# Three edits to a transformer block's kernel: an 8-bit copy of the quantised values, later attention transposes, later waits for right factors

## The chip, the cores and the metric

The kernel runs on one core of one Trainium2 chip. The metric is the device time of one execution in microseconds. TensorE (PE) does the matrix products and the transposes, VectorE (DVE) and ScalarE (ACT) the elementwise work, SyncE (SP) issues most of the DMAs, and GpSimd (POOL) does six reductions across partitions. Each engine works through its own list of instructions in order. What one engine needs from another is guarded by semaphores: an instruction that waits holds back all that stands behind it in the list of its engine.

## The reference, cut to what matters

`x` has 16 batches of 64 tokens of 1024 numbers. Three blocks, each fed with the layernorm of `x`, are added to it one after another.

```python
x = x + xattn(layernorm(x), ctx, ctx, ...)     # cross attention over 1601 context rows, batch norm
x = x + attn(layernorm(x), Wq, Wk, Wv, Wo, ...)
x = x + ffn(layernorm(x), W1, b1, W2, b2)

# attn: 8 heads with two softmax maps each
q = (x @ Wq).reshape(B, T, 8, 2, 64); k = (x @ Wk).reshape(B, T, 8, 2, 64)
v = (x @ Wv).reshape(B, T, 8, 128)
o = softmax(mask(q0 k0^T)/8) v - lam * softmax(mask(q1 k1^T)/8) v
o = o * rsqrt(mean(o*o) + eps) * g * (1 - LAMBDA_INIT)
out = o.reshape(B, T, E) @ Wo

# ffn: weights made ternary (alpha * sign(W) where |W| > 0.05 max|W|), then
y = gelu(x @ W1q.T + b1) @ W2q.T + b2
scale = max|y| / 7 + 1e-8
out = clip(round(y / scale), -7, 7) * scale
```

## The kernel before, in words

The kernel is written by hand as one list of instructions for each engine. The order inside each list is the order of the code. The 1024 tokens lie in `NT = 8` tiles of 128 partitions, and the 1024 features in `NC = 8` chunks.

**Attention.** The loop over the heads `h` runs from 0 to `H - 1 = 7` and is a software pipeline: while PE makes the queries and keys of head `h`, the softmax and the weighing of the values of head `h - 1` pass through DVE and ACT. The queries and keys of a head come from seven block products (a scheme in the manner of Strassen), `qk_product(h, m)` with `m` from 0 to 6 (line 943), each of four f32 matrix instructions of 512 columns, which the profile counts as eight records. Product 0 goes to PSUM bank 0, 1 to bank 1, 2 to bank 0, 3 to bank 2, 4 to bank 0, 5 to bank 3, 6 to bank 0. Between them PE does three pieces for the head before: `turn(h)` transposes the attention weights `a_bd` (line 953), `weigh(h)` multiplies them by the values (line 963), and `put_oT(h)` transposes the normalised result (line 971). Then `scores(h)` makes the 64 small score products (line 982): its start waits for DVE's last collection of the head (`dve_part`), its second half for ACT's copy `part(h, 6)` (`act_part >= 3h + 3`).

The list of ACT for one head is: `exps(h)` (line 615, with a table load ahead of it), `part(h, 0)` and `part(h, 1)` (copies of products 0 and 1 out of PSUM, line 639), `count(4h)`, `put_aT(h)` (line 620), `squares(h)` (line 626, then a table load and a small square root at line 628), `count(4h + 1)`, `count(4h + 2)`, `part(h, 6)`, `put_oT(h)` (line 633), `count(4h + 3)`. A `count` is three passes over a 128x1024 tile of W1 (lines 607, 609, 611).

The list of DVE for one head is: `shift(h)` (lines 1368 to 1371), `right_sum_4(h)`, `ternary(4h)` (lines 1325 and 1326), `combine(h)` (lines 1375 to 1383, the last of which writes `a_bd`), `collect_qk(h, 0)`, `ternary(4h + 1)`, `collect_qk(h, 1)`, `ternary(4h + 2)`, `normal(h)` (line 1387 to 1393; inside it `collect_qk(h, 2)`), `right_sums(h + 1)`, `collect_qk(h, 3)`, `ternary(4h + 3)`. A collection (line 1403) adds a bank of PSUM to the queries or keys.

`ternary(n)` needs the tile `n` of W1 in one of two buffers `w_buf`. SP loads tile `n + 2` into the buffer of tile `n` (line 424) when `count(n)` is done.

**The product with W2.** It is also made from seven block products, `product(r, s)` with `r` from 0 to `7 * HK - 1 = 111` and four row groups `s` (line 1075). Step `r` needs a left factor in the ring `hl` (written by ACT and DVE) and a right factor in the ring `t_half` of 8 slots, which SP loads from DRAM when step `r - 8` is done (line 480). `operands(r)` holds the two waits. The last eight steps are ordered the other way round: all eight for `s = 0`, then all eight for `s = 1`, and so on, so that DVE can collect row group 0 while PE does the others (lines 1527 and 1531).

**The end.** DVE and POOL find the largest `|y|` over all. For each of the 8 tiles the value `y / scale` is then rounded by adding `ROUND = 1.5 * 2**23` and taking it off again, multiplied by the scale and added to `xo2`. ACT does the first pass for tiles 1 to 7 (line 709) and DVE for tile 0 (line 1557). Taking `ROUND` off is done by ACT for the tiles in `Q_ACT = (2, 4, 6, 7)` (line 713) and by DVE for 0, 1, 3 and 5 (line 1563). DVE multiplies and adds (line 1565), and SP stores each tile to DRAM (line 504).

Of the kernel before, what the change touches and what calls it, by code (L numbers as in the profile page):

```python
# [26 lines left out]

F32 = mybir.dt.float32
F16 = mybir.dt.float16
ALU = mybir.AluOpType  # L30
ACT = mybir.ActivationFunctionType
AX = mybir.AxisListType
# [2 lines left out]
P = 128  # L35
B, C, N = 16, 64, 1024
M = 1601
NT = B * C // P
# [32 lines left out]
ROUND = 1.5 * 2.0 ** 23  # L71
QMAX = 7.0
Q_ACT = (2, 4, 6, 7)
H_ORDER = [(hc, j) for j in range(2) for hc in range(4)] + [(hc, j) for hc in range(4, HC) for j in range(2)]
HK = HC // 2
RING = 12
BRING = 8
LAST_K = 8
# [27 lines left out]
def build(nc, x, ctx, ctxT_in, small_w, wqk, wv, wo, lambdas, w1t, w2t, b2, consts, out):  # L106
    with ExitStack() as stack:
# [3 lines left out]
        def sb(name, shape, at, dt=F32):  # L111
            return nc.alloc_sbuf_tensor_at(name, shape, dt, offset=BASE + at)

        KB = 1024
# [23 lines left out]
        x2T = sb("x2T", [P, NC, NT * P], 84 * KB)  # L138
        t_out = sb("t_out", [P, 2, 1024], 116 * KB, F16)
        tok = sb("tok", [P, NT, N], 120 * KB)  # L140
# [9 lines left out]
        x3s = [sb("x3s0", [P, N], 48 * KB), sb("x3s1", [P, N], 116 * KB)]  # L150
        x3h = sb("x3h", [P, NC, NT * P], 160 * KB, F16)
        x3l = sb("x3l", [P, NC, NT * P], 176 * KB, F16)

        w2_buf = sb("w2_buf", [P, 2, 1024], 0)
        t2_set = sb("t2_set", [P, 2, 8, BANK], 8 * KB, F16)
        hl = sb("hl", [P, RING, 2, BANK], 0, F16)
        t_half = sb("t_half", [P, BRING, BANK], 24 * KB, F16)
        hq = sb("hq", [P, 4, HK, BANK], 32 * KB)
        xo2 = sb("xo2", [P, NT, N], 96 * KB)
        y = sb("y", [P, NT, N], 160 * KB)  # L160
        t_buf = sb("t_buf", [P, 4, 1024], 192 * KB, F16)
        b2_bc = sb("b2_bc", [P, N], 200 * KB)

        at = [204 * KB]

        def small(name, shape):
            n = 4 * int(np.prod(shape[1:]))
            t = sb(name, shape, at[0])
            at[0] += n + (-n) % 32
            return t  # L170
# [25 lines left out]
        ym = small("ym", [P, 24])  # L196
# [82 lines left out]
        whole_ready = sem("whole_ready")  # L279
        z_ready, q_ready, d_vec, out_stored = sem("z_ready"), sem("q_ready"), sem("d_vec"), sem("out_stored")  # L280
# [29 lines left out]
        def width(mt):  # L310
            return P if mt < MT - 1 else TAIL
# [213 lines left out]
        def _(act):  # L525
            A = act.activation
# [17 lines left out]
            for p in range(NT):  # L544
# [3 lines left out]
                for e, pair in enumerate(pairs(p)):  # L548
                    n = BANK if pair[0] == "wide" else 4 * width(pair[0])
# [32 lines left out]
            for hf in range(2):  # L582
                f = slice(hf * BANK, hf * BANK + BANK)
# [101 lines left out]
            for m, (hc, j) in enumerate(H_ORDER):  # L685
# [5 lines left out]
                if m >= 1 and H_ORDER[m - 1] in T2_AFTER:  # L691
                    n = T2_AFTER[H_ORDER[m - 1]]
# [12 lines left out]

            act.wait_ge(d_vec, 2)

            def rounded(t):
                A(y[:, t, :], y[:, t, :], ACT.Copy, scale=ym[:, 20:21], bias=ROUND).then_inc(z_ready, 1)

            def whole(t):
                act.wait_ge(z_ready, t)
                A(y[:, t, :], y[:, t, :], ACT.Copy, bias=-ROUND).then_inc(whole_ready, 1)

            for t in range(NT):
                if t > 0:
                    rounded(t)
                if t in Q_ACT:
                    whole(t)


        @block.tensor
        def _(pe):
# [193 lines left out]
            def qk_product(h, m):  # L917
                b = (0, 1, 0, 2, 0, 3, 0)[m]
                if m == 0:
                    pe.wait_ge(wqk_in[(h + 1) % 2], 16 * (h // 2) + 16)  # L920
                    if h:
                        pe.wait_ge(act_part, 3 * h)
                if h == 0 and m in (0, 1, 3, 5):
                    pe.wait_ge(v_out, 2 * NT - 3 + b)
                if h == 0 and m in (1, 2, 4, 5):
                    pe.wait_ge(xs_sum, 4 * (1, 2, 4, 5).index(m) + 4)
                if m == 1:
                    pe.wait_ge(tw_ready, 4 * h + 3)
                if m == 2:
                    pe.wait_ge(act_part, 3 * h + 1)  # L930
                if m == 3 and h:
                    pe.wait_ge(dve_part, 4 * h - 2)
                if m == 4:
                    pe.wait_ge(dve_part, 4 * h + 1)
                if m == 5 and h:
                    pe.wait_ge(dve_part, 4 * h)
                if m == 6:
                    pe.wait_ge(dve_part, 4 * h + 3)
                    pe.wait_ge(tw_ready, 4 * h + 4)
                fresh = m in (0, 1, 3, 5)  # L940
                for c in range(4):
                    right, left = factors(h, m, c)
                    ins = mm(bank(b), right, left, start=(fresh and c == 0), stop=(c == 3), skip_group_check=not fresh)  # L943
                ins.then_inc(m_done, 1)
# [40 lines left out]

            pe.wait_ge(x2_out, 2 * NT)
            for h in range(H):
                for m in range(3):
                    qk_product(h, m)
                if h:  # L990
                    turn(h)
                qk_product(h, 3)
                if h:
                    weigh(h)
                for m in range(4, 7):
                    qk_product(h, m)
                if h:
                    put_oT(h)
                    pe.wait_ge(on_ready, h)
                scores(h)  # L1000
# [64 lines left out]
            def product(r, s):  # L1065
                m, k = r // HK, r % HK
                b = 4 * (m % 2) + s
                if k == 0:
                    if m < 2:
                        pe.wait_ge(g_ready, 2 * HC - 7 + b)  # L1070
                    else:
                        pe.wait_ge(y_out, 4 * (m - 2) + s + 1)
                fresh = m in (0, 1, 3, 5)
                for n in range(2):
                    ins = mm(bank(b), hl[:, r % RING, n, s * P:s * P + P], t_half[:, r % BRING, :],  # L1075
                             start=(fresh and k == 0 and n == 0), stop=(k == HK - 1 and n == 1),
                             skip_group_check=not fresh)
                if k == HK - 1:
                    ins.then_inc(y_done, 1)
                return ins  # L1080

            def operands(r):
                pe.wait_ge(b_in[r % BRING], 16 * (r // BRING + 1))
                pe.wait_ge(lo_ready, r + 1)

            for n in range(7 * HK - LAST_K):
# [2 lines left out]
                    ins = product(n, s)  # L1089
                if n % HK < HK - 1:  # L1090
                    ins.then_inc(k_used, 1)
            for n in range(7 * HK - LAST_K, 7 * HK):
                operands(n)
            for s in range(4):
                for n in range(7 * HK - LAST_K, 7 * HK):
                    product(n, s)


        @block.vector
        def _(dve):  # L1100
            V = dve

            def inverse_root(own, v, root, inv, tmp):

                own.done(V.reciprocal(inv, root))
                own.done(V.tensor_tensor(tmp, inv, inv, ALU.mult))
                own.done(V.tensor_tensor(tmp, tmp, v, ALU.mult))
                own.done(V.tensor_scalar(tmp, tmp, -0.5, 1.5, ALU.mult, ALU.add))
                own.done(V.tensor_tensor(inv, inv, tmp, ALU.mult))

            own = Own(V, vec)

            def stats(q):
# [6 lines left out]
                own.done(V.bn_aggr(mv[:, q, :], st[:, 0:2, :]))  # L1120
                V.tensor_scalar(rs[:, 0, 0:1], mv[:, q, 1:2], EPS, None, ALU.add).then_inc(var_ready, 1)

            def make_x1(q):
                V.wait_ge(root_ready, q + 1)
                inverse_root(own, rs[:, 0, 0:1], rs[:, 1, 0:1], rr[:, 0, q:q + 1], t8[:, 0:1])
                if q >= 2:
                    V.wait_ge(n_stored, 16 * (q - 1))
                V.tensor_scalar(x1s[:, q % 2, :], x_t[:, :], mv[:, q, 0:1], rr[:, 0, q:q + 1], ALU.subtract, ALU.mult)\
                    .then_inc(x1s_ready, 1)
# [25 lines left out]
            for p in range(NT):  # L1155
# [5 lines left out]
                for e, pair in enumerate(pairs(p)):  # L1161
                    n = BANK if pair[0] == "wide" else 4 * width(pair[0])
# [36 lines left out]
                for u, mts in enumerate(units):  # L1199
                    n, nt = width(mts[-1]), len(mts)  # L1200
                    V.wait_ge(at_ready, U * p + u + 1)
                    t = bank(unit_bank(u), nt * AW)[0:n, :].rearrange("p (t a) -> p t a", a=AW)
# [3 lines left out]
                    s = slots[mts[0]]  # L1206
# [309 lines left out]
            bias = lambda col: b2_bc[:, BANK * col:BANK * col + BANK]  # L1516
# [18 lines left out]
            for r in range(RING, 7 * HK + 2):  # L1535
                if r // HK in sums:
                    sums[r // HK](r % HK)
                if r >= RING + 2:
                    n = r - 2
# [14 lines left out]

            for t in range(NT):
                if t == 0:
                    own.done(V.tensor_scalar(y[:, 0, :], y[:, 0, :], ym[:, 20:21], ROUND, ALU.mult, ALU.add))
                else:
                    V.wait_ge(z_ready, t)
                if t in Q_ACT:  # L1560
                    V.wait_ge(whole_ready, Q_ACT.index(t) + 1)
                else:
                    own.done(V.tensor_scalar(y[:, t, :], y[:, t, :], -ROUND, None, ALU.add))
                for f in [slice(0, N)] if t < NT - 1 else [slice(0, BANK), slice(BANK, N)]:
                    V.scalar_tensor_tensor(xo2[:, t, f], y[:, t, f], ym[:, 19:20], xo2[:, t, f], ALU.mult, ALU.add)\
                        .then_inc(q_ready, 1)


# [42 lines left out]
```

## Time and profile before

| what | value |
|---|---|
| time, median of 3 runs | 1420.54 us (1419.92 to 1421.53) |
| time of the profiled execution | 1418.05 us |
| span of the profiled execution, first to last instruction | 1416.2 us |
| PE busy | 1357.6 us (96%) |
| DVE busy | 820.5 us (58%) |
| ACT busy | 512.7 us (36%) |
| mean granted clock of TensorE | 0.986 of full speed |

The span is the time from the first to the last instruction; 1.85 us of the profiled execution lie around it. Busy time counts an instruction from its start to its end, and matrix instructions overlap each other by a little, so that the times of consecutive groups on PE can overlap by 0.1 to 0.2 us.

### The profile page before, as it was taken

What the parts mean: (1) busy time and instruction counts of PE and PEld (TensorE: products, weight loads), DVE (VectorE), ACT (ScalarE), POOL (GpSimd) and SP (SyncE); (2) the same over time, 40 slices, a digit from 0 to 9 for tenths busy, and PEclk for the clock granted to TensorE, in tenths of its full rate; (3) what the DMA queues carried; (4) which work ended last, traced back from release to release, by engine and by line L of the source; (5) the groups of instructions that cost most, each with busy time, mean ns of one, the idle gap of its engine ahead of it and who ended that gap; (6) DMA issues with size and microseconds to landing.
All of it is one profiled execution on the core that took longest, in us unless ns stands there. A gap on an engine that the chain in (4) does not pass through costs nothing.

```text
span 1416.2 us, 17052 instructions
## 1 busy us (share of the span) xinstructions
PE 1357.6 (96%) x6642; PEld 646.0 (46%) x6642; DVE 820.5 (58%) x1409; ACT 512.7 (36%) x790; POOL 2.4 (0%) x10
## 2 busy tenths in 40 slices
PE   6979999999999969999999999999999999999993
PEld 4535435444454434444555555444444444444441
DVE  3223424234242288787888885765677853566955
ACT  1111203113021122117777774102666665333333
POOL 0000000000000000000000000000000000000000
PEclk9989999999999989999999999999999999999997
DMA  9999999999989687854444436342778761222263
GB/s 383 420 421 420 421 421 422 404 396 410 382 327 404 247 301 263 306 193 149 131 152 164 148 120 267 119 135 89 209 236 240 238 195 41 79 75 78 75 194 126
DMA packets 110719, 347.01 MB, mean 245 GB/s; under 512 B 40624, under 2 KB 55344, under 8 KB 85040
## 3 DMA queue, kind: packets, MB, share of 16 engines
q1 hardware_dynamic: 107472, 334.38, 64.5%
q10 hardware_dynamic: 3168, 11.54, 2.0%
q8 instruction: 54, 0.88, 0.3%
q14 instruction: 25, 0.20, 0.0%
HBM read 304.47 MB, written 41.42 MB: 244 GB/s over the span
## 4 chain that ended last, share of the span: by engine, by line
PE 66%; issue 16%; DVE 9%; DMA 7%; ACT 2%; SPq 0%; DVEq 0%; POOLq 0%; POOL 0%
PE ps L1060 15%; PE ps L841 12%; PE ps L1010 8%; PE ps L751 7%; PE ps L943 6%; PE ps L897 5%; DMA ctx_sb<-in_ctx 5%; PE ps L793 4%; PE ps L772 4%; PE ps L823 2%; DMA w_scan<-in_w2t 1%; PE ps L963 1%; DVE t_out L1326 1%; DMA w_buf<-in_w1t 1%; PE ps L775 1%
## 5 line engine op out<-in xcount | busy, mean ns | idle before, releaser
L1075 PE MATMUL ps<-t_half,hl 128*128 128x512 f16 x896 | 193.7, 379 | 2.2 <-DMA t_half<-t_dram 2.2
L841 PE MATMUL ps<-ctx_sb,attnT 128*64 128x512 f32 (+1 forms) x832 | 183.5, 601 | 4.4 <-DMA ctx_sb<-in_ctx 4.4
L553 ACT ACTIVATE stg<-ps 128x512 f32<-128x512 f32 (+1 forms) x80 | 44.3, 554 | 356.6 <-PE ps L772 312.7
L1075 PEld LDWEIGHTS ps<-t_half,hl 128*128 128x128 f16 x896 | 87.6, 98 | 108.2 <-issue 2.7
L1060 PE MATMUL ps<-x3h,t_buf 128*128 128x512 f16 x512 | 121.0, 379 | 0.0
L1060 PE MATMUL ps<-x3l,t_buf 128*128 128x512 f16 x512 | 120.9, 379 | 0.0
L751 PE MATMUL ps<-ctxT,x1T 128*64 128x512 f32 x512 | 116.4, 599 | 0.6 <-DMA ctxT<-in_ctxT 0.6
L841 PEld LDWEIGHTS ps<-ctx_sb,attnT 128*64 128x64 f32 (+1 forms) x832 | 59.8, 138 | 122.0 <-issue 115.2
L1496 DVE TENSOR_TENSOR hl<-hq,hl 128x512 f16<-128x512 f32 x112 | 76.3, 689 | 66.6 <-ACT hl L683 66.2
L897 PE MATMUL ps<-wv_sb,x2T 128*128 128x512 f32 x256 | 112.0, 596 | 0.0
L1010 PE MATMUL ps<-wo_sb,oT 128*128 128x512 f32 x256 | 111.6, 593 | 0.3 <-ACT oT L633 0.3
L683 ACT ACTIVATE hl<-hq 128x512 f16<-128x512 f32 x112 | 70.1, 628 | 108.5 <-PE ps L1075 97.1
L1166 DVE COPY stg<-ps 128x512 f32<-128x512 f32 (+1 forms) x80 | 50.8, 638 | 87.6 <-PE ps L772 69.9
L1141 DVE SCALAR_TENSOR_TENSOR x1s<-ps,sw,x1s 128x512 f32<-128x512 f32 x16 | 12.0, 751 | 146.0 <-PE ps L841 146.0
L943 PE MATMUL ps<-xs,tw 128*128 128x512 f32 x192 | 85.0, 592 | 0.0
L1219 DVE TENSOR_REDUCE wmx<-w_scan 128x1 f32<-128x1024 f32 x64 | 75.2, 1213 | 14.2 <-DMA w_scan<-in_w2t 7.9
L688 ACT ACTIVATE hq<-ps,sw,al 128x512 f32<-128x512 f32 x64 | 49.8, 778 | 80.2 <-PE ps L1060 80.2
L1060 PEld LDWEIGHTS ps<-x3l,t_buf 128*128 128x128 f16 x512 | 50.1, 98 | 60.4
L1060 PEld LDWEIGHTS ps<-x3h,t_buf 128*128 128x128 f16 x512 | 50.0, 98 | 60.1 <-DMA t_buf<-t_dram 0.4
L897 PEld LDWEIGHTS ps<-wv_sb,x2T 128*128 128x128 f32 x256 | 48.4, 192 | 58.1 <-issue 58.1
L1010 PEld LDWEIGHTS ps<-wo_sb,oT 128*128 128x128 f32 x256 | 47.9, 190 | 57.6 <-issue 56.9
L793 PE MATMUL ps<-stg,x1T 128*64 128x65 f32 (+2 forms) x608 | 71.1, 375 | 0.0
(198 smaller groups left out, 1596.8 us busy)
## 6 DMA issues: line engine op xcount, KB each, us to landing
ctxT<-in_ctxT SPq DMA_DIRECT2D x64, 1024.0 KB, 16.3
ctx_sb<-in_ctx SPq DMA_DIRECT2D x16, 4096.0 KB, 21.8
ctx_sb<-in_ctx SPq DMA_DIRECT2D x16, 2048.0 KB, 11.6
w_scan<-in_w1t SPq DMA_DIRECT2D x32, 512.0 KB, 5.8
w_buf<-in_w1t SPq DMA_DIRECT2D x32, 512.0 KB, 3.7
w_scan<-in_w2t SPq DMA_DIRECT2D x32, 512.0 KB, 5.6
w_buf<-in_w2t SPq DMA_DIRECT2D x32, 512.0 KB, 4.1
t_dram<-t_set SPq DMA_DIRECT2D x16, 1024.0 KB, 6.5
```

The costliest lines, as they stand in the source:

```text
L683: A(hl[:, r % RING, 0, :], hq[:, LEFT[m], k, :], ACT.Copy).then_inc(hi_ready, 1)
L751: ins = mm(bank(ea + g, m1 - m0)[C * b:C * b + C, :], x1T[:, q % 2, c, C * b:C * b + C], ctxT[:, k % SLOTS, b, m0:m1], start=(c == 0), sto ...
L772: ins = pe.transpose(bank(pair_bank(p, e, b))[:, i * P:i * P + P], ctx_sb[:, 8 + i, b, a * P:a * P + P], ident)
L793: ins = mm(out[C * b:C * b + C, :], x1T[:, p % 2, c, C * b:C * b + C], stg[:, e % 4, b, i * w:i * w + w], start=(c == 0), stop=(c == NC - 1))
L841: ins = mm(bank(ea + hf)[C * b:C * b + C, :], attnT[0:w, slots[mt], C * b:C * b + C], ctx_sb[0:w, mt, b, hf * BANK:hf * BANK + BANK], star ...
L897: ins = mm(bank(2 * (t % 2) + hf), x2T[:, c, t * P:t * P + P], wv_sb[:, c, hf * BANK:hf * BANK + BANK], start=(c == 0), stop=(c == NC - 1))
L943: ins = mm(bank(b), right, left, start=(fresh and c == 0), stop=(c == 3), skip_group_check=not fresh)
L1010: ins = mm(bank(2 * (t % 2) + hf), oT[:, c, t * P:t * P + P], wo_sb[:, c, hf * BANK:hf * BANK + BANK], start=(c == 0), stop=(c == H - 1))
L1060: ins = mm(bank(b), t_buf[:, hc % 4, c * P:c * P + P], part[:, c, j * BANK:j * BANK + BANK], start=(c == 0 and n == 0), stop=(c == NC - 1 ...
L1075: ins = mm(bank(b), hl[:, r % RING, n, s * P:s * P + P], t_half[:, r % BRING, :], start=(fresh and k == 0 and n == 0), stop=(k == HK - 1 a ...
L1219: V.tensor_reduce(wmx[:, n // WT, n % WT:n % WT + 1], buf[:, n % 4, :], AX.X, ALU.max, apply_absolute_value=True).then_inc(scanned, 1)
L1496: V.tensor_tensor(hl[:, r % RING, 1, :], left(r // HK, r % HK), hl[:, r % RING, 0, :], ALU.subtract)\
```

## The change

There are three edits.

1. **The end.** A new tile `z` of 8-bit whole numbers takes the place of the first pass's result. The conversion to 8 bits does the rounding, so the pass that takes `ROUND` off goes, on ACT and on DVE alike. `z` lies at 192 KB in the space of `t_buf`, which is no longer used by then.
2. **Attention.** For heads 1 to 7 PE does `qk_product(h, 3)` before `turn(h)` and not after it, and `qk_product(h, 4)` before `weigh(h)` and not after it. For head 0 the order stays.
3. **The last eight steps of the product with W2.** The eight pairs of waits no longer stand ahead of the first product of row group 0, but each ahead of its own.

```diff
+I8 = mybir.dt.int8
...
+        z = sb("z", [P, NT, N], 192 * KB, I8)
...  (ACT, the end)
-            def rounded(t):
-                A(y[:, t, :], y[:, t, :], ACT.Copy, scale=ym[:, 20:21], bias=ROUND).then_inc(z_ready, 1)
-
-            def whole(t):
-                act.wait_ge(z_ready, t)
-                A(y[:, t, :], y[:, t, :], ACT.Copy, bias=-ROUND).then_inc(whole_ready, 1)
-
-            for t in range(NT):
-                if t > 0:
-                    rounded(t)
-                if t in Q_ACT:
-                    whole(t)
+            for t in range(1, NT):
+                A(z[:, t, :], y[:, t, :], ACT.Copy, scale=ym[:, 20:21]).then_inc(z_ready, 1)
...  (PE, attention)
             for h in range(H):
-                for m in range(3):
+                for m in range(4):
                     qk_product(h, m)
                 if h:
                     turn(h)
-                qk_product(h, 3)
+                qk_product(h, 4)
                 if h:
                     weigh(h)
-                for m in range(4, 7):
+                for m in range(5, 7):
                     qk_product(h, m)
                 if h:
                     put_oT(h)
...  (PE, the last eight steps)
-            for n in range(7 * HK - LAST_K, 7 * HK):
-                operands(n)
             for s in range(4):
                 for n in range(7 * HK - LAST_K, 7 * HK):
+                    if s == 0:
+                        operands(n)
                     product(n, s)
...  (DVE, the end)
                 if t == 0:
-                    own.done(V.tensor_scalar(y[:, 0, :], y[:, 0, :], ym[:, 20:21], ROUND, ALU.mult, ALU.add))
+                    own.done(V.tensor_scalar(z[:, 0, :], y[:, 0, :], ym[:, 20:21], None, ALU.mult))
                 else:
                     V.wait_ge(z_ready, t)
-                if t in Q_ACT:
-                    V.wait_ge(whole_ready, Q_ACT.index(t) + 1)
-                else:
-                    own.done(V.tensor_scalar(y[:, t, :], y[:, t, :], -ROUND, None, ALU.add))
                 for f in [slice(0, N)] if t < NT - 1 else [slice(0, BANK), slice(BANK, N)]:
-                    V.scalar_tensor_tensor(xo2[:, t, f], y[:, t, f], ym[:, 19:20], xo2[:, t, f], ALU.mult, ALU.add)\
+                    V.scalar_tensor_tensor(xo2[:, t, f], z[:, t, f], ym[:, 19:20], xo2[:, t, f], ALU.mult, ALU.add)\
                         .then_inc(q_ready, 1)
```

## Rows read from the trace of the kernel before

**Rows 1.** Busy us (instructions) by stretch: PE, PEld, DVE, ACT, POOL; clock; DMA share; GB/s.

```profile
711.10:740.50 29.40, 29.06 (x158) 15.05 (x152) 24.29 (x33) 22.21 (x32) 0.00 (x0) 1.00 0.45 143
...
1369.00:1398.00 29.00, 25.63 (x119) 11.28 (x116) 12.73 (x19) 2.13 (x4) 0.00 (x0) 1.00 0.35 110
```

**Rows 2.** Waits of PE for DVE in attention: total, times, longest.

```profile
PE ps L953 <- DVE a_bd L1383: 2.3, 7, 0.3
```

**Rows 3.** Timeline of a head from its weighing on: start, length, instruction.

```profile
698.74 3.60 PE L943 MATMUL ps<-xs,tw 128*128 128x512 f32 x8
...
698.94 1.02 ACT L626 ACTIVATE o_sq<-ps 128x1024 f32<-128x1024 f32 x1 [4.57 <-PE ps L963]
...
702.37 0.69 DVE L1403 TENSOR_TENSOR kT<-ps,kT 128x512 f32<-128x512 f32 x1 [0.96 <-PE ps L943]
...
704.02 1.22 DVE L1393 TENSOR_TENSOR o_n<-ps,rs 128x1024 f32<-128x1024 f32 x1
...
707.09 0.68 DVE L1403 TENSOR_TENSOR kT<-ps,kT 128x512 f32<-128x512 f32 x1
...
708.28 0.19 ACT L611 ACTIVATION_READ_ACCUMULATOR w_buf<-t_out 128x1 f32 x1
...
708.97 0.75 DVE L1325 TENSOR_SCALAR t_out<-w_buf,thr 128x1024 f16<-128x1024 f32 x1 [1.20 <-DMA w_buf<-in_w1t]
709.04 1.04 PE L971 MATMUL ps<-cst,o_n 128*128 128x128 f32 x8
...
709.24 0.60 ACT L639 ACTIVATE qT<-ps 128x512 f32<-128x512 f32 x1 [0.77 <-PE ps L943]
...
710.01 1.16 PE L982 MATMUL ps<-kT,qT 64*64 64x64 f32 x64
```

**Rows 4.** Timeline of the first part of the next head.

```profile
711.10 3.70 PE L943 MATMUL ps<-x2T,wqk_a 128*128 128x512 f32 x8
711.24 1.23 DVE L1368 TENSOR_TENSOR sm<-ps,cst 128x1024 f32<-128x1024 f32 x1 [0.19 <-PE ps L982]
...
714.64 7.03 PE L943 MATMUL ps<-xs,tw 128*128 128x512 f32 x16
...
716.86 0.58 ACT L639 ACTIVATE qT<-ps 128x512 f32<-128x512 f32 x1
...
720.54 1.40 DVE L1383 TENSOR_TENSOR a_bd<-sm 64x512 f32<-64x512 f32 x2
...
722.00 1.09 PE L953 MATMUL ps<-cst,a_bd 128*128 128x128 f32 x8 [0.34 <-DVE a_bd L1383]
...
722.93 3.60 PE L943 MATMUL ps<-x2T,wqk_a 128*128 128x512 f32 x8
```

**Rows 5.** Timeline at the last eight steps of the product with W2.

```profile
1378.96 2.04 SPq L480 DMA_DIRECT2D t_half<-t_dram  x2
1382.90 3.40 PE L1075 MATMUL ps<-t_half,hl 128*128 128x512 f16 x15 [2.24 <-DMA t_half<-t_dram]
```

**Rows 6.** Timeline of the end.

```profile
1399.58 0.75 DVE L1557 TENSOR_SCALAR y<-y,ym 128x1024 f32<-128x1024 f32 x1
1400.37 0.69 DVE L1563 TENSOR_SCALAR y<-y 128x1024 f32<-128x1024 f32 x1
...
1409.25 3.80 DVE L1565 SCALAR_TENSOR_TENSOR xo<-y,ym,xo 128x1024 f32<-128x1024 f32 x4
```

**Rows 7.** Groups of the end: count, then busy us, mean ns, idle before.

```profile
L1565 DVE SCALAR_TENSOR_TENSOR xo<-y,ym,xo 128x1024 f32<-128x1024 f32 x7 | 8.7, 1281 | 0.1
L709 ACT ACTIVATE y<-y,ym 128x1024 f32<-128x1024 f32 x7 | 7.7, 1135 | 25.2 <-DVE ym L1553 25.2
```

**Rows 8.** DMA in the last 8.2 us: GB/s in 40 slices, stores, us to landing.

```profile
GB/s 0 300 440 380 420 380 440 360 420 400 440 400 400 340 0 0 240 380 440 380 420 380 440 380 420 400 420 380 400 300 410 380 360 400 370 360 20 0 0 0
...
out<-xo SPq DMA_DIRECT2D x3, 512.0 KB, 2.7
out<-xo SPq DMA_DIRECT2D x2, 256.0 KB, 2.8
```

## The prediction

> **What bounds the kernel now.** I read the share of busy time first: PE is busy for 1357.6 of 1416.2 us, so a change pays only where it shortens PE's list, closes one of its gaps, or lies behind its last product. Then I took the busy time by stretch. A head of attention lasts 29.40 us, of which PE is busy 29.06, DVE 24.29 and ACT 22.21 [rows 1]; the other full heads are alike (six of the seven stretches are 29.40 or 29.41 us, one 29.50). So PE leaves only 0.34 us open in each head, and the list of waits puts that down to DVE's `a_bd`: 2.3 us in 7 times [rows 2]. That gap is what the second edit can win. The timeline of one head [rows 3, 4] shows what each engine does in that time, and above all how much room ACT and DVE have; the reader is to see there that ACT's copy `part(h, 6)` starts 0.77 us after ACT came free, so ACT is behind PE by almost nothing to spare. At the last eight steps PE stands still once, for 2.24 us [rows 5]. After the last product the chain runs through DVE and ends with a store [rows 6, 8].
>
> **Edit 2, attention.** Call o the moment at which `weigh(h)` leaves PE: 698.74 in the head shown [rows 3]. The edit moves nothing off any engine. It moves the transposes behind product 3, and the weighing behind product 4. So of the three products (4, 5, 6) that used to follow the weighing only two are left. These three were the cover for what ACT has to do between o and `scores`.
>
> *ACT's path from o.* The squares start at 698.94; then come the table load, the square root and two counts; the second count ends at 708.28 + 0.19 = 708.47 [rows 3]. None of this depends on PE. `part(h, 6)` takes 0.60 [rows 3], so it is done at 709.07, and PE can go on at about 709.15 (0.08 for the semaphore, an estimate between the 0.06 from the end of `a_bd`, 721.94, to the transposes [rows 4] and twice that).
>
> *PE's path from o, before.* Three products bring it to 709.04, `put_oT` to 710.01, the scores to 711.10 [rows 3, 4].
>
> *PE's path from o, after.* Products of (709.04 - 698.74) / 3 = 3.43 us each: two of them end at 705.61. `put_oT` (0.97) needs `o_n`, before done at 704.02 + 1.22 = 705.24, in time. It ends at 706.58. The scores need collection 3, before done at 707.77; it comes some 0.9 us sooner, because collection 2 no longer waits 0.96 for product 4 [rows 3], so at about 706.9: 0.3 us of waiting. The first half of the scores (0.55) is done at 707.4, and the second half must wait for ACT until 709.15. The scores end at 709.70, where PE alone would have ended at 706.58 + 1.09 = 707.67. **This is a new wait of 2.03 us in every head from 1 to 7.**
>
> *A second wait follows.* After count(4h + 1) the next load of `w_buf` is started; it is there at 708.97 [rows 3], 10.2 us after o, and DVE's last ternary tile of the head ends 2.07 later, at 711.04. None of these times hangs on PE, so they stay where they are relative to o, while the scores end 1.40 earlier (709.70 against 711.10). Hence `shift` can start no sooner than before (711.2, [rows 4]), ACT's last count too, and then the exponentials. `part(h, 0)`, which stands behind the exponentials in ACT's list, still ends at 716.86 + 0.58 = 717.44. But PE is at the door of product 2, which overwrites the bank that this copy reads, at 709.70 + 3.54 + 3.44 = 716.68. It waits until 717.52: **0.84 us in each of heads 2 to 7.**
>
> *What the edit wins.* `a_bd` is done at 721.94, as before. Product 2 now ends at 717.52 + 3.44 = 720.96, product 3 at 724.40, so the transposes no longer wait. They take 0.93 (722.00 to 722.93, [rows 4]), product 4 follows to 728.77, the weighing (1.78) to 730.55. From o to o that is 31.81 us, against 29.41: **+2.40 us a head.**
>
> *Sum.* In head 1 the weighing comes 3.44 us later, less the gap of 0.48 between the end of product 2 at 721.52 and the transposes (its 0.34 of waiting and a seam): +2.96. Six more heads give 6 x 2.40 = 14.4. Behind the last weighing two products and the stall stand for three products: 10.96 for 12.36, -1.40. Together **+16.0 us**. Behind the last scores PE has 28 products of the projection (28 x 0.43 = 12.0 us) ahead of the transposes of the last head, so it comes to them 10.96 + 12.0 = 23.0 after o. `a_bd` is done 721.94 - 698.74 = 23.2 after o in the head shown, where a ternary tile more stands before it than after the last head; so there is a wait of 0.3 at most there, and I count none. Low bound of the whole edit: only the first wait, with nothing from the second, 7 x (2.03 - 0.48) = +10.9. High bound: collection 3 keeps its old time (707.77) and all semaphores cost 0.2 instead of 0.08, 0.3 more a head, +18.
>
> **Edit 3, the last eight steps.** PE was ready at 1382.90 - 2.24 = 1380.66, and waited for the last right factor, whose load was issued at about 1380.7 as the second of two [rows 5]. With the waits spread out, steps 0 to 6 of row group 0 go ahead: 7 x 2 products of 0.2155 (3.40 us for 15 and the overlap, [rows 5]) keep PE going to 1383.68, and the factor is there at 1382.90. The margin is 0.78 us, so the whole wait goes: **-2.24**. If the loads came a microsecond later it would be -2.0; the bound below is 0. Behind it DVE's collections (two passes over 512 columns each, under 0.8 us a pass) still fit inside the 3.45 us of eight steps of a row group.
>
> **Edit 1, the end.** DVE sets the pace: tile 0 has a first pass (0.75), the pass that takes `ROUND` off (0.69) and the final one (1.28) [rows 6, 7]; in all it has 4 passes of the second kind, and it ends at 1409.25 + 3.80 = 1413.05. Without them: 1400.37 for the first final pass, seven at a pace of 1.24 (1.281 less an overlap of 0.04), and two halves (3.80 - 2 x 1.24 = 1.32): 1410.37, so DVE ends 2.68 earlier. ACT delivers a tile in 1.135 and starts with it [rows 7], faster than 1.24, and its second passes go as well; it isn't late anywhere. Now the stores: 512 KB at 400 to 440 GB/s [rows 8] take 1.28 us, a hair more than DVE's 1.24. The first store is issued at 1401.68 and lands 2.7 later, 1404.38; seven more at 1.28 give 1413.34, against 1410.40 + 2.8 = 1413.2 by DVE. So the stores end 1413.34, where they ended 1413.05 + 0.05 + 2.8 = 1415.9: **-2.5** (2.56, and something for the seams between stores).
>
> An 8-bit output isn't in the trace. The nearest rows are the same operation with f32 output (0.69 to 0.75) and with f16 output at `ternary` (0.75, [rows 3]), so I take 0.75; upwards I bound it by DVE's slowest pass over as many elements, 1.28, which would make the first tile 0.5 us later: -2.0. Only tile 0 would pay. For the final pass, already at 1.28 with f32, I see no gain or loss from reading 8 bits.
>
> The store rate is where a page speaks against the edit. The rows show 400 to 440 GB/s in full slices of the end [rows 8]. The Trainium skill, "DMA: Bandwidth & Descriptors", section "Where 436 GB/s comes from", says that between HBM and on-chip memory the HBM side binds at about 358 GB/s. By that figure 4.19 MB would take 11.7 us and the end would win some 1.4 us less, an estimate; the trace disagrees with it here, so the sum goes by the rows.
>
> **Sum.** Against the profiled execution (1418.05): +16.0 - 2.24 - 2.5 = +11.3, so 1429.3. The median of the runs shown is 2.49 higher than that execution, 1420.54, so I forecast **1431.8 us**, slower by 0.8%.
>
> **Rivals.**
>
> *A, the scores don't wait for ACT (faster).* Place: the second half of `scores`. PE is at that half 706.58 + 0.55 = 707.13, 8.4 us after o, and `part(h, 6)` would have to be done by then; the rows say 10.3 [rows 3]. It decides from the point on where the wait is under 0.48 in a head. If there is no new wait, the edit wins the old one, 7 x 0.34 = 2.4, and the time is 1420.54 - 2.4 - 2.24 - 2.5 = 1413.4. For it: PE is 99% busy and ACT 76%, so by shares there is room. Against it: ACT's list is strictly in order, and nothing in it between o and that copy goes away. 4%.
>
> *B, the first wait alone.* If ACT gets through the exponentials sooner, because `shift` can start when the scores end, product 2 doesn't wait. Then +10.9 - 4.74 = +6.2, 1426.7. For it: ternary tiles may find their buffer earlier than I think. Against it: the 10.2 us from o to the buffer are ACT's own work and one load, all on record. 12%.
>
> *C, the clock.* The new stalls (2 us and 0.8 us) could cost clock. Price: one product of each head at 1.2 GHz instead of 2.4, +3.4 x 7 = +24, 1456. Against it: the stall of 2.24 us lies in a stretch with a granted clock of 1.00 [rows 1, 5], as all heads do. 3%.
>
> *D, the 8-bit pass isn't what it looks like, or the waits of edit 3 stay.* +0.5 or +2.2: 1432.3 or 1434.0. 8%.
>
> **How the numbers follow.** My own case has 73%. Its range is 1427.5 (both waits 0.4 us smaller in each head and the end at its best) to 1435 (the high bound of edit 2). With D inside, and the lower part of B, the range 1426 to 1436 leaves out A, C and a little of B: under 2 in 10. A measurement of this kernel tells about 0.2% from nothing, 2.8 us. Faster: A, 4%. Within 0.2% (1417.7 to 1423.4): it would take half the stalls that I find, 3%. Slower: 93%.
>
> **What the profile after would show.** The seven waits of the transposes (line 953) are gone. In their place the scores (line 982) wait for ACT's copy at line 639 (or the whole group stands idle between line 971 and the next head) by about 2 us in 7 heads, and the second group of products (line 943) for ACT's copy by 0.8 in 6. A head lasts 31.8 us instead of 29.4. ACT's copy `part(h, 6)` has no idle time before it any more, and DVE's wait for `w_buf` at line 1325 grows. The wait of 2.24 us before the last eight steps is gone. At the end lines 713 and 1563 are missing, DVE's last pass ends some 10.8 us after it begins, and the stores are back to back. The prediction is wrong if the heads keep under 30 us: then ACT isn't in the way where I put it.

## The result, and the profile after

The changed kernel takes 1434.92 us (median of 4 runs, 1432.07 to 1435.55), against 1420.23 us for the kernel before in the same comparison. The ratio is 1.0098, with a 95% interval from 1.0081 to 1.0116: 1% slower, by 14.7 us (the difference of the medians; by the ratio it is 13.9). The forecast was 1431.8 us. The profiled execution took 1435.55 us, with a span of 1433.7.

The edits move the line numbers: on PE and DVE they are 8 lower than before (the products of attention, 943, are now 935, the transposes 945, the scores 974), on ACT and SP 2 higher (ACT's copy of products 0 and 6, 639, is now 641). Behind the passes that are gone DVE's lines move further: its final pass, 1565, is now 1553.

The list of TensorE's waits in attention, with total, times and the longest, answers to [rows 2] (the last row is the first product of the output projection, right behind the last scores):

```profile
PE ps L974 <- ACT qT L641: 10.1, 7, 1.7
PE ps L935 <- ACT qT L641: 5.2, 5, 1.5
PE ps L974 <- DVE kT L1395: 1.4, 6, 0.2
PE ps L935 <- DVE kT L1395: 1.0, 1, 1.0
PE ps L1002 <- issue: 0.5, 1, 0.5
```

The transposes no longer stand in it: their 2.3 us are gone. The scores (line 974) wait for ACT's copy of product 6 in all 7 heads, and in six for DVE's last collection. The products (line 935) wait for ACT's copy of product 0 in five of the six heads. That is 16.7 us of waiting for 2.3. (The fourth row is head 0's, which had 0.4 before; it is between 0.4 and 1.7 in the traces with the old order of attention too.)

The timeline of one head, from its weighing on, answers to [rows 3, 4]; o is 706.20 here:

```profile
706.20 3.60 PE L935 MATMUL ps<-xs,wqk_b 128*128 128x512 f32 x8
706.40 1.02 ACT L628 ACTIVATE o_sq<-ps 128x1024 f32<-128x1024 f32 x1 [4.57 <-PE ps L955]
...
709.63 3.63 PE L935 MATMUL ps<-x2T,tw 128*128 128x512 f32 x8
...
713.10 1.04 PE L963 MATMUL ps<-cst,o_n 128*128 128x128 f32 x8
...
714.36 0.69 PE L974 MATMUL ps<-kT,qT 64*64 64x64 f32 x32 [0.22 <-DVE kT L1395]
...
715.83 0.58 ACT L641 ACTIVATE qT<-ps 128x512 f32<-128x512 f32 x1
...
716.47 0.69 PE L974 MATMUL ps<-kT,qT 64*64 64x64 f32 x32 [1.41 <-ACT qT L641]
716.55 0.76 DVE L1317 TENSOR_SCALAR t_out<-w_buf,thr 128x1024 f16<-128x1024 f32 x1 [2.33 <-DMA w_buf<-in_w1t]
...
718.54 1.22 DVE L1360 TENSOR_TENSOR sm<-ps,cst 128x1024 f32<-128x1024 f32 x1
...
724.44 0.58 ACT L641 ACTIVATE qT<-ps 128x512 f32<-128x512 f32 x1
...
725.07 3.70 PE L935 MATMUL ps<-xs,tw 128*128 128x512 f32 x8 [0.85 <-ACT qT L641]
...
732.04 1.04 PE L945 MATMUL ps<-cst,a_bd 128*128 128x128 f32 x8
```

Two products follow the weighing, then `put_oT`, then half of the scores; the copy of product 6 runs directly behind ACT's counts, with no idle time before it, from 9.63 us after o on, where it ran 10.50 after o, and after 0.77 of idling, before. The scores' second half begins when it is done. DVE's last ternary tile waits 2.33 us for its buffer (1.20 before), so `shift` starts at 718.54, 12.34 after o, although the scores end 10.9 after o. The exponentials, and with them the copy of product 0 (724.44), come 18.2 after o as they did before, and product 2 waits 0.85 us. The transposes at 732.04 wait for nothing.

The busy time of this head by stretch (the columns as in [rows 1]), and six stretches of 2 us around two of the scores' waits:

```profile
706.20:738.14 31.94, 29.46 (x155) 15.09 (x153) 24.17 (x33) 22.01 (x32) 0.00 (x0) 1.00 0.41 132
...
812.00:814.00 2.00, 0.88 (x33) 0.81 (x34) 0.75 (x1) 2.00 (x5) 0.00 (x0) 0.96 0.89 266
814.00:816.00 2.00, 2.00 (x3) 0.86 (x3) 1.97 (x3) 0.87 (x2) 0.00 (x0) 0.50 0.63 238
816.00:818.00 2.00, 2.00 (x4) 0.72 (x3) 1.93 (x3) 1.94 (x4) 0.00 (x0) 0.69 0.35 131
...
878.00:880.00 2.00, 1.49 (x30) 0.87 (x23) 1.96 (x3) 1.00 (x3) 0.00 (x0) 0.67 0.03 8
880.00:882.00 2.00, 2.00 (x4) 0.90 (x3) 1.97 (x2) 1.97 (x3) 0.00 (x0) 0.50 0.70 152
882.00:884.00 2.00, 2.00 (x5) 0.76 (x4) 1.83 (x4) 1.95 (x5) 0.01 (x1) 0.97 0.68 231
```

A head lasts 31.94 us, against 29.40; the others last 31.89 to 32.61. The column of the granted clock shows what the head's sum doesn't: twice, behind the scores' wait of one head and behind that of the last, the clock was at 0.50, which is 1.2 GHz, for about 3.4 us. The missing share is 2 x (0.04 + 0.50 + 0.31) = 1.70 us the first time and 2 x (0.33 + 0.50 + 0.03) = 1.72 the second. The first fall cost the head only 0.6 us (32.52 for 31.94), because the slow product 0 ended when product 2 would have had to wait anyway; that head is the one without the second wait.

At the last eight steps of the product with W2 no wait of TensorE is left. The timeline of the end, which answers to [rows 6], and the stores in the last 12.7 us, which answer to [rows 8]:

```profile
1419.48 7.39 ACT L711 ACTIVATE z<-y,ym 128x1024 int8<-128x1024 f32 x7 [22.76 <-DVE ym L1545]
1419.48 0.75 DVE L1549 TENSOR_SCALAR z<-y,ym 128x1024 int8<-128x1024 f32 x1
1420.27 9.79 DVE L1553 SCALAR_TENSOR_TENSOR xo<-z,ym,xo 128x1024 f32<-128x1024 int8 x9
1421.59 9.37 SPq L506 DMA_DIRECT2D out<-xo  x9
```

```profile
GB/s 0 0 0 0 232 400 413 400 400 413 413 387 413 413 413 413 387 426 413 387 387 413 413 400 387 413 413 413 400 413 387 413 393 355 393 374 387 136 0 0
...
out<-xo SPq DMA_DIRECT2D x7, 512.0 KB, 3.0
out<-xo SPq DMA_DIRECT2D x2, 256.0 KB, 3.3
```

The pass with 8-bit output takes 0.75 us, and the final pass 1.28 as before. The nine final passes follow each other without a gap, and the stores too, at about 400 GB/s; a store now lands 3.0 to 3.3 us after its issue instead of 2.7 to 2.8, presumably because it waits for the one before it; the rows don't name what a store waits for. From the start of TensorE's last product to the end of the span it takes 17.3 us instead of 19.7.

**Where the 17.5 us of the two spans are.** The starts of the stages in both traces give: +1.4 ahead of the attention heads (1.2 of them because the stage of the values took 118.0 us for 116.8), +0.7 in head 0, +18.1 in heads 1 to 7, +0.5 of idling and +1.6 of low clock between the last scores and the next transposes, 0 in the projection and the product with W1, -2.4 in the product with W2, and -2.4 at the end.

The 1.2 us of the values are clock as well, and have nothing to do with the edits. The stage begins at 509.3 us before and at 509.6 after, each time at a clock of 0.50, behind about 9 us in which TensorE had next to nothing to do; what differs is when the clock rises. PE busy, clock, DMA share and GB/s, before and then after:

```profile
510.00:514.00 4.00, 4.00 (x9) 0.89 0.33 131
510.00:514.00 4.00, 4.00 (x6) 0.57 0.32 131
```

The missing share is 4 x 0.11 = 0.4 us before and 4 x 0.43 = 1.7 after. The late rise stands in 6 of the 13 traces of this study (after, `e2`, `e5`, `e7`, `e9`, `e11`), and in exactly these the stage takes longer, by 1.0 to 1.5 us; edits of every kind are on both sides.

### The profile page after: what moved, and what is told of

Its sections match the earlier page's. It is cut to its first block, busy times and chain, and to the rows that moved or that the text cites. A ratio compares the mean times of both kernels' runs of the same rounds, so it can differ in the third digit from the quotient of the medians.

```text
span 1433.7 us, 17040 instructions
## 1 busy us (share of the span) xinstructions
PE 1362.6 (95%) x6642; PEld 648.6 (45%) x6642; DVE 817.1 (57%) x1405; ACT 507.2 (35%) x786; POOL 2.4 (0%) x10
## 4 chain that ended last, share of the span: by engine, by line
PE 66%; issue 15%; DMA 8%; DVE 5%; ACT 5%; SPq 0%; DVEq 0%; POOLq 0%; POOL 0%; ACTq 0%
PE ps L1052 15%; PE ps L833 12%; PE ps L1002 8%; PE ps L743 7%; PE ps L935 6%; PE ps L889 5%; DMA ctx_sb<-in_ctx 4%; PE ps L785 4%; PE ps L764 4%; DMA w_buf<-in_w1t 2%; PE ps L815 2%; DMA w_scan<-in_w2t 1%; ACT w_buf L611 1%; ACT w_buf L613 1%; ACT w_buf L609 1%
```

## The experiments

All are compared with runs of the kernel before on the same chip: 1419.50 us for `e1` to `e4`, 1419.32 for `e5`, `e6`, `e8` and `e9`, 1420.16 for `e7`, `e10` and `e11`. Where an experiment is set against the changed kernel, that is its median of 1434.92 us, which was taken in another comparison, so such a difference is rougher by about 1 us.

**The change in parts.** `e1` has the new order of attention alone, `e2` all but that (so the first and the third edit), `e3` the 8-bit values alone, `e4` the late waits of the last eight steps alone. The diffs are those parts of the change.

> The kernel before with the second edit alone. Theory (the two ACT waits of a head, and a lower clock behind some of them): +16 us for the waits and 1 to 4 us for the clock, so +17 to +20 us against the kernel before; a head lasts 31.9 us. Rival (the waits alone, clock of no account): +16.0 us and equal heads of 31.8 us. Rival (the slower attention comes from the other two edits, through the placement of the code): about 0.

> The changed kernel with the old order in attention, so the first and third edit alone. Theory: -2.24 - 2.5 = -4.7 us against the kernel before, heads of 29.4 us. Rival (the store rate or the late right factor takes part of it back): -2 to -3 us.

> The kernel before with the 8-bit values alone. Theory: -2.5 us, the stores back to back at about 410 GB/s. Rival (HBM binds at a lower rate of about 358 GB/s): -1.1 us.

> The kernel before with the waits of the last eight steps spread out, alone. Theory: -2.24 us, and no wait of TensorE after 1195 us. Rival (the last right factor is still late when it is asked for): 0 to -1 us.

| kernel | median us | ratio, 95% interval | us against before |
|---|---|---|---|
| e1 | 1438.02 | 1.0132 (1.0118 to 1.0147) | +18.7 |
| e2 | 1413.82 | 0.9959 (0.9946 to 0.9971) | -5.8 |
| e3 | 1418.72 | 0.9993 (0.9984 to 1.0002) | -1.0 |
| e4 | 1416.30 | 0.9981 (0.9972 to 0.9990) | -2.7 |

(The last column is the ratio's.) So the whole loss is the second edit's, 18.7 us, and the other two together win 5.8, somewhat more than the 4.7 forecast. The two results add up to +12.9, for the 13.9 (by the ratio) of all three. In `e1` the heads last 31.8 to 32.1 us, and one stretch of low clock, behind the last scores, costs 1.7 us.

`e3` fell short of its -2.5 by the medians, but its trace shows the 2.4 us at the end in full: 17.4 us from the last product's start to the end, against 19.7. In that execution 1.7 us were lost again elsewhere: the old wait for the right factor, 2.38 us there, was followed by low clock (stretches of 2 us, columns as above):

```profile
1382.00:1384.00 2.00, 0.00 (x0) 0.00 (x0) 0.00 (x0) 0.00 (x0) 0.00 (x0) 1.00 0.32 98
1384.00:1386.00 2.00, 1.96 (x6) 0.78 (x7) 0.00 (x0) 0.00 (x0) 0.00 (x0) 0.65 0.04 8
1386.00:1388.00 2.00, 2.00 (x6) 0.76 (x5) 0.00 (x0) 0.00 (x0) 0.00 (x0) 0.50 0.00 0
```

2 x (0.35 + 0.50) = 1.7 us are lost there, and the product with W2 took 197.4 us instead of 195.6. In the traces of the kernel before (2.24 us) and of `e1` (2.40 us) the same wait cost no clock.

For the medians that is no explanation. The mean granted clock of `e3`'s 11 executions is 0.98573, that of the 21 of the kernel before 0.98495, and an end that is shorter by 2.4 us at a clock of 0.50 accounts for this difference by itself (2.4 x 0.5 / 1417 = 0.0008). So `e3` lost no more clock than the kernel before, and why its executions gained only 1.0 us (between 2.3 gained and 0.3 lost by the interval) stays open. What the same means do show is the price of the old wait: with that wait gone and the end as before, `e4` has 0.98564 over 11 executions, 0.0007 or 1.0 us of the span better than the kernel before. That is an estimate, good to some 0.5 us, from clocks listed to 0.001. It fits the -2.7 of `e4`, and `e2`, whose 0.98680 is 0.0010 or 1.4 us above what the shorter end alone gives: 2.2 + 2.4 + 1.4 = 6.0 for its 5.8. The intervals (about 1.3 us each way for `e3` and `e4`, 1.8 for `e2`) would allow `e2` to exceed the sum of the two without a cause, too.

**Which of the two waits sets the head.** In `e5` ACT's copy of product 6 no longer stands behind the third count. In `e6` the copy of product 0 stands ahead of the exponentials as well. Both are made from the changed kernel:

```diff
 (ACT, e5 and e6)
                 count(WH * h + 1)
-                count(WH * h + 2)
+                if not h:
+                    count(WH * h + 2)
                 part(h, 6, qT[:, BANK:2 * BANK], 0)
                 if h:
                     put_oT(h)
+                    count(WH * h + 2)
                 count(WH * h + 3)
 (ACT, e6 alone)
+                part(h, 0, qT[:, 0:BANK], 0)
                 if h:
                     exps(h)
-                part(h, 0, qT[:, 0:BANK], 0)
```

> The changed kernel with ACT's copy of product 6 and its two copies of the transposed result moved ahead of the third count, for heads 1 to 7. Theory of the prediction (two waits in a row, the second set by ACT's exponentials, which are set by the load of the W1 buffer): the scores no longer wait for ACT, but product 2 now waits 2.6 us for the copy of product 0 in place of 0.8, a head stays at 31.8 to 31.9 us, and the time is that of the changed kernel within 2 us. Rival (the scores' wait is the cause by itself): 7 x 2 = 14 us come back, 1421 us.

> As e5, and the copy of product 0 stands ahead of the exponentials and no longer behind them. Theory: both waits go but for 0.3 to 0.5 us; a head lasts 29.6 to 29.7 us, the transposes don't wait, and the time is 3 to 4 us under the kernel before, about 1417. Rival (the transposes' new place costs by itself, through the chain from the weighing to the next weighing): a head stays over 31 us, 1428 or more.

`e5` took 1439.98 us, ratio 1.0148 (1.0132 to 1.0164): nothing came back, and it is even 5 us slower than the changed kernel, 3 more than the 2 that I had allowed. TensorE's waits in its attention, up to the last scores (the products are line 937 here, the scores 976; the first row is product 2 in heads 2 to 7, the second is head 0's):

```profile
PE ps L937 <- ACT qT L641: 15.0, 6, 2.7
PE ps L937 <- DVE kT L1397: 1.5, 1, 1.5
PE ps L976 <- DVE kT L1397: 1.4, 6, 0.2
```

The scores' wait for ACT is gone, and none of it came back: the wait is now all before product 2, 2.5 us a time. A head without a fall of the clock lasts 32.2 us, and 33.6 with one: the clock was low behind five of the six waits, 8.5 us in all, which is where the excess comes from. The mean granted clocks agree: 0.981 to 0.983 in its four executions, 0.983 to 0.988 in the changed kernel's. The timeline shows one, a group of products of 5.40 us instead of 3.6:

```profile
720.52 3.60 PE L937 MATMUL ps<-xs,tw 128*128 128x512 f32 x8
726.67 5.40 PE L937 MATMUL ps<-xs,tw 128*128 128x512 f32 x8 [2.55 <-ACT qT L641]
```

`e6` took 1416.90 us, ratio 0.9985 (0.9975 to 0.9995), 2.1 us under the kernel before and 18 under the changed one, with heads of 29.4 to 30.4 us and no low clock in the attention; product 2 still waits for ACT in four heads, 1.7 us in all and 0.9 the longest, for the 0.3 to 0.5 that I had expected. So both waits come from where ACT's two copies stand, and the second takes over what is saved on the first. The copy of product 0 alone wasn't moved, so what the first wait costs without the second is not shown.

The transposes of the last head, which stand behind 28 products of the output projection, wait for DVE's `a_bd` once in these variants: 1.3 us in `e5`, 1.0 in `e6`, 1.1 in `e9`. In the changed kernel they don't wait.

**Which work of ACT counts.** `e8` and `e9` cut one of a head's four counts to 32 of 1024 columns, the second and the third; the rest of those tiles isn't counted.

```diff
-                w = w_buf[n % 2][:, :]
+                few = slice(0, 32 if n > WH and n % WH == 1 else 1024)   # e9: == 2
+                w = w_buf[n % 2][:, few]
```

> The changed kernel with the second count of each head from 1 to 7 cut to 32 of 1024 columns: the rest of that tile isn't counted, so the scale of W1 is off. Theory: this count stands in both chains, ahead of the copy of product 6 and ahead of the load that the last ternary tile waits for; 2.6 us less of it remove nearly all of both waits, a head lasts 29.1 to 29.4 us, and the time is 1413 to 1417 us. Rival (the waits come from the order on TensorE, whatever ACT does): over 31 us a head.

> The changed kernel with the third count of each head from 1 to 7 cut to 32 of 1024 columns: the rest of that tile isn't counted, so the scale of W1 is off. Theory: this count stands only ahead of the copy of product 6, and not in the chain over the load; so the scores' wait goes, product 2 waits 2.4 us or so instead, and a head stays at 31.8 us, as in e5. Rival (ACT is simply too busy between the weighing and the scores): the same gain as with the second count cut, heads under 30 us.

Each ran once: `e8` 1415.12 us, `e9` 1437.21 us. The waits of TensorE are the cleaner measure. In `e8` the only ones left are 1.3 us for DVE's last collection and 0.8 in head 0; a head lasts 29.5 us (0.1 over the range that I had given). In `e9`, whose ACT has as much less to do, they are these:

```profile
PE ps L936 <- ACT qT L642: 15.0, 6, 2.6
PE ps L975 <- DVE kT L1396: 1.3, 6, 0.2
PE ps L936 <- DVE kT L1396: 0.6, 1, 0.6
```

They are the waits of `e5`, with heads of 31.9 to 33.8 us. 2.6 us less work on ACT bring the head back to 29.5 us in the one place and do nothing for it in the other; the two kernels are 22 us apart. The second count stands ahead of the load of the W1 buffer and so of the last ternary tile, of `shift` and of the exponentials; the third doesn't.

**Which half of the new order costs.** `e10` keeps the transposes behind product 3 and puts the weighing right behind them. `e11` puts the transposes back behind product 2 and leaves the weighing behind product 4.

```diff
 (e10)                                   (e11)
                 for m in range(4):                      for m in range(3):
                     qk_product(h, m)                        qk_product(h, m)
                 if h:                                   if h:
                     turn(h)                                 turn(h)
                     weigh(h)                            for m in range(3, 5):
                 for m in range(4, 7):                       qk_product(h, m)
                                                         if h:
                                                             weigh(h)
                                                         for m in range(5, 7):
```

> Of the changed kernel's attention only the transposes stay behind product 3, and the weighing follows them at once, with three products behind it again. Theory (what counts is how many products stand between the weighing and the scores): no wait of the scores for ACT, no wait of product 2, only some 0.4 us for ACT's copy of the transposes; a head lasts 29.4 to 29.5 us, the time is about 1414 to 1415 us. Rival (a late transpose costs by itself): over 30 us a head.

> The transposes stand in their old place, the weighing behind product 4, with two products behind it. Theory: all waits of the changed kernel (scores 1.4 to 1.6 us, product 2 0.85 us) and one more, since the transposes ask for the attention weights 1 us too soon; a head lasts 32.8 us, which with some low clock gives 1439 to 1446 us. Rival (the place of the transposes is what costs): heads of 29.4 us, 1414 us.

`e10` took 1415.12 us, ratio 0.9963 (0.9951 to 0.9975); its heads last 29.44 us, and the weighing waits for ACT's `aT` (2.4 us in 7). `e11` took 1437.38 us, ratio 1.0125 (1.0111 to 1.0138); its heads last 32.6 to 33.4 us, with these waits:

```profile
PE ps L974 <- ACT qT L641: 10.2, 7, 1.7
PE ps L935 <- ACT qT L641: 6.4, 6, 1.5
PE ps L945 <- DVE a_bd L1376: 3.4, 7, 0.5
```

The late transposes by themselves cost nothing; the late weighing costs all. The third line is the wait that the edit was to remove, and it came back as 0.5 a head, less than the 1 us that I had expected of it. The time, 1437.38, is under the 1439 that I had given as the least: in its profiled execution no stretch of the attention had a low clock, for all its waits, and the mean granted clock of its four executions is 0.986 to 0.988.

**A version that beats both.** `e7` has the first and third edit, the old order of attention, and DVE's fourth right sum behind the combination:

```diff
 (DVE, from the kernel without the second edit)
                     shift(h)
-                    right_sum_4(h)
                 ternary(WH * h)
                 if h:
                     combine(h)
+                    right_sum_4(h)
```

> The first and third edit with the old order in attention, and DVE's fourth right sum moved from behind the shift to behind the combination, so that the last step of the attention weights comes 0.6 us sooner. Theory: the one gap of 0.34 us per head closes, a head lasts 29.1 us, 2.4 us less than with the first and third edit alone: 1411 to 1412 us, and no wait of the transposes for DVE. Rival (another wait stands right behind it, the collection ahead of the scores or the buffer of W1): heads of 29.3 us or more, 1413 to 1414 us.

1411.10 us, ratio 0.9935 (0.9922 to 0.9949): 9.2 us under the kernel before (by the ratio) and 24 under the changed one. The busy time of one head by stretch:

```profile
711.10:740.20 29.10, 29.02 (x153) 15.06 (x152) 24.37 (x34) 22.29 (x33) 0.00 (x0) 1.00 0.45 144
```

TensorE stands idle for 0.08 us in it; the wait for the attention weights is down from 2.3 us in 7 heads to 0.2 in one.

## Why the prediction was right, point by point

**The first wait, 2.03 us a head: right in place, a little high.** The kernel after shows 0.22 for the last collection and 1.41 for ACT, 1.63 together. ACT's path from o to the end of the copy is 10.21 us, for 10.33 forecast, and the scores end 10.89 after o, for 10.96. So TensorE resumes when I said; the difference is in how the profile counts the rest: each interruption shows a tail of the product before it as busy (PE's busy time of a head rose from 29.06 to 29.46 us with the same instructions). `e5`, `e8` and `e9` show that it is ACT's list that TensorE waits for.

**The second wait, 0.84 us a head: right**, 0.85 in the head shown, and so is its cause: `e8` and `e9` single out the chain from the second count through the load of the buffer, the last ternary tile, `shift` and the exponentials. The trace shows it once more by chance. In the head after the one shown the load was slower, DVE's ternary tile waited for it 3.00 us in place of 2.33, and product 2 waited 1.52 in place of 0.85: the same 0.67 both times, and a head of 32.61 us. What I missed is this: with the wait in place, every delay of that load is TensorE's own. The true weight of the second chain is also greater than 0.84: without the first wait it grows to 2.5 and keeps the head as long as it was (`e5`).

**The head of 31.81 us: right**, 31.89 and 31.94 where neither the load nor the clock is late. The +16.0 of the edit came out at +18.1 in heads 1 to 7; the slower loads (0.67 and two of 0.1 to 0.2) and the net 0.6 of the first fall of the clock account for 1.5 to 1.7 of the 2.1.

**The clock (rival C) is where most of the rest lies.** I gave it 3% and a price of 24 us, as one case for all heads. It is neither all nor nothing: behind some of the waits TensorE ran at 1.2 GHz for about 3.4 us, at up to 1.7 us each. My evidence against it, that the wait of 2.24 us in the trace of before left the clock at 1.00, was one draw: in `e3` the same wait did cost the clock, in `e1` it didn't. The spans of the two profiled executions differ by 17.5 us where the sum said 11.3. Of the 6.2 between them, 2.1 are those of the heads, 2.1 lie behind the last scores (0.5 of idling that the profile doesn't explain, 1.6 of clock), and 2.1 are in the values (1.2, the late rise of the clock), ahead of them and in head 0, where nothing was changed. So 1.2 us of the miss of the spans are chance, and this rival had no term for a clock that differs between executions of one kernel. The medians differ by 14.7, since the profiled execution of the kernel before was 2.2 us below the median of this comparison and that of the changed kernel 0.6 above. How the parts stand in the executions without a trace isn't known, but the fastest of the changed kernel, 1432.07 us, is also the one with the highest mean clock, 0.988 against 0.983 to 0.985. The largest thing that the sum lacks is thus the clock, which it put at nothing: 0.6, 1.6 and 1.2 us of the 6.2. The two waits and both gains have their forecast size within 0.4 us each.

**Edit 3, -2.24: right**, with -2.4 in the product with W2 in every trace that has it, and -2.7 (interval -4.0 to -1.4) by the times of `e4`; the clock that the old wait cost in some executions would make it about 3.2, and the interval holds both. **Edit 1, -2.5: right**, -2.4 in every trace that has it. The 8-bit output costs nothing extra (0.75 us), and the stores are the new limit of the end, as reckoned: about 400 GB/s rather than 410, so 0.1 to 0.2 us later, and over the 358 GB/s of the Trainium skill, "DMA: Bandwidth & Descriptors", section "Where 436 GB/s comes from". That the time of `e3` shows only 1.0 of it stays open, as said above; between `e4` and `e2`, which has edit 1 on top, it is 3.1.

**Rivals A, B and D** didn't occur. A would have needed ACT's path to be 1.9 us shorter. B said that the second wait might not be there; it was, in five of the six heads, and in the sixth the low clock took its place. D's two parts are answered by the 8-bit pass of 0.75 us and by the last eight steps without a wait.

## What to carry to other kernels

Before a step is moved later to close a small gap, measure what stood behind it as cover. Here one product fewer between the weighing and the scores uncovered ACT's list (22.2 us busy of 29.4, but in strict order and with 0.77 us to spare at the place that mattered), and 2.3 us of waiting turned into 16.7. A wait that vanishes when its cause is moved (`e5`) can stand again at the next consumer of the same chain; so follow the chain from one occurrence of a step to the next, and shorten that (`e7` took 0.6 us of DVE work out of it and closed the gap). And a wait of TensorE of 1.4 us can cost more than its length, in clock. Before a time difference of a microsecond or two is put down to an edit, compare the granted clock of the stages that the edit doesn't touch.

## What the runs showed of the hardware that I had not expected

TensorE's granted clock can fall to 0.50 for about 3.4 us behind a wait as short as 1.4 us, at a cost of 1.7 us, and whether it does differs from wait to wait and from run to run. In the profiled execution of the changed kernel it fell behind one of the six scores' waits of 1.41 us (0.7 us after its end, behind 32 small score products), and behind the seventh, of 1.70 us, which has another 0.51 of idling behind it, and not behind a product's wait of 1.52; in `e1` behind the seventh alone; in `e11` behind none of seven; behind 5 of the 6 waits of 2.5 us in `e5` and 4 of 6 in `e9`; and, of the waits of 2.2 to 2.4 us for the right factor, behind that of `e3` and not behind those of the kernel before and of `e1`. So the waits of 2.2 us and more lost it more often, in 10 cases of 15, than those of 1.4 to 1.7 us, in 3 of 25 over all traces. But length isn't all: the longest wait of `e5`, 2.71 us, didn't lose it, and of the waits for the right factor 2.38 us lost it and 2.40 didn't. The Trainium skill, "TensorE: Matmul & The Clock Gate", section "HAM oscillation — how this bites in real kernels", describes a clock that falls after idle gaps and costs half of the time until it is back; the rows agree with the half, 1.7 of 3.4 us, and what decides whether a given short wait triggers it stays open here.
